# Window attention on one core: first batch in smaller pieces, the first strip's v masked by ScalarE, the projection turned later, and a wait moved from the pooled out to two other places

## The chip, the cores and the metric

The kernel runs on one core of a Trainium2 chip. The metric is the device time of one execution in microseconds (us). A core has five instruction queues: PE (TensorE), DVE (VectorE), ACT (ScalarE), POOL (GpSimd) and SP (SyncE, which here only issues DMAs). They run side by side and meet at semaphores.

## What is computed

The input x is (4, 128, 96, 96) float32. It goes through a group norm of 32 groups, then a linear attention over windows of 4x4 pixels, once on the windows and once on their 5x5 averages, and a projection with a batch norm; x is added at the end.

```python
qkv = jnp.einsum('nchw,oc->nohw', xw, qkv_w)            # xw: windows of 4x4 pixels
pooled = _avg_pool5(qkv)
msq = jnp.concatenate([qkv, pooled], axis=1)            # 32 heads of 3*8 channels
q, k, v = relu(msq[..., :8]), relu(msq[..., 8:16]), msq[..., 16:]
v = jnp.pad(v, ..., constant_values=1.0)                # the ones give the denominator
kv = jnp.einsum('ngld,nglm->ngdm', k, v)
out = jnp.einsum('ngld,ngdm->nglm', q, kv)
out = out[..., :-1] / (out[..., -1:] + 1e-15)
y = jnp.einsum('nchw,oc->nohw', out, proj_w)            # then the batch norm
x = x + y                                               # the attention gets _gn(x)
```

## The kernel before

Each of the 4 images of the batch is cut into 24 strips of four rows, so there are 96 strips (NS), each of 384 columns with the 128 channels on the partitions. All of x stays in x_all. SP loads batch 0 in six DMAs of four strips, then the constants and weights (all five on loaded_w), and the later batches two strips at a time.

**Head.** DVE takes the statistics of each strip as it lands (L453), and works out mean and reciprocal deviation in a chain of small operations (L461 to L488). It then normalises strip 0 (L517) and pools it (L509). POOL does both for strip 1 and every later strip (L286, L292, L264). ScalarE's two square roots (L407) serve this chain and the batch norm's scale (L629 to L637), by which DVE multiplies the projection's weights; PE turns these through PSUM (L811) and DVE copies them out to projT (L644). The columns of ones in vm_pool are written by DVE (L641), those of vm_full come with the DMA below.

**A strip's stages.** PE multiplies the normalised strip with the k and v weights (conv_kv, L659; for the pooled pixels conv_kv_pooled, L668) into PSUM banks 2, 3 and 6. ScalarE takes k out through a relu (relu_k L344, relu_k_pooled L349). v must stand in vm_full and vm_pool once per window of a quad, with zeros in the other windows' rows. For the full pixels ScalarE copies v once (copy_v, L355) and SP spreads it with four DMAs of every fourth row (spread_v, L234). For the pooled pixels ScalarE writes six masked copies, each with a column of constants as scale (masked_v_pooled, L366). PE then multiplies k with v (kv_products and kv_products_pooled, L687, in tiles of 64 rows and 32 columns), DVE copies the result out under a mask of own heads (own_heads, L561), PE multiplies with q (out_products and out_products_pooled, L703: 48 products of one strip each, that is 96 matmul records), DVE divides (L592 to L596), PE transposes (L778) and ScalarE copies out (L391, L398). In project PE multiplies with projT, first the full part (L787, bank 0) and then the pooled one (L789, bank 1). DVE adds the full part to x_all (residual, L567), ScalarE copies the pooled part to y_pool (copy_y_pooled, L403), between the second and third of the six masked copies, and POOL adds it (residual_pooled, L264). SP stores the strip.

**Order.** PE's step for strip s is written out by hand:

```python
conv_kv(s + 1, p); transposes(s - 1); conv_kv_pooled(s + 1, p)
project(s - 1, out_next=True)
out_products(s); out_products_pooled(s)
kv_products(s + 1); kv_products_pooled(s + 1)
conv_q(s + 1, p)
```

It stands in a hardware loop over strips 1 to 94, two to a turn, with strip 0 ahead of it and strip 95 behind. ScalarE's order in a step is relu_q, relu_q_pooled, copy_v, to_image, pooled_out, relu_k, relu_k_pooled, then the six masked copies. In the loop, out_products_pooled(s) begins with a wait for added_f (DVE has added the full part of strip s - 1) and y_copied (ScalarE has copied its pooled part) on an instruction that does nothing else. kv_products(s + 1), which writes banks 0 and 1, waits for vm_f alone. In twelve steps out of 96 DVE also has a part of the next batch's statistics between its own work (phases 0 to 3).

Of the kernel before, what the change touches and what calls it, by code (L numbers as in the profile page):

```python
# [11 lines left out]
P = 128  # L12
Q4 = 32
WS = 4
D = 8
# [21 lines left out]
C_TP = C_VP + EP  # L37
C_PACK = C_TP + EP
N_CONST = C_PACK + P


def constants():


    c = np.zeros((P, N_CONST), np.float32)
    p = np.arange(P)
    c[:, C_IDENT:C_IDENT + P] = np.eye(P)
    quad, head = p // Q4, p % Q4 // D
    for j in range(QG):
        at = C_OWN + j * KC  # L50
        c[:, at:at + KC] = (quad[:, None] % QG == j) & (head[:, None] == np.arange(KC)[None] // HC)
    win_p = p % Q4 // PXP
    side = np.array([1, 2, 1])
    times = (side[:, None] * side[None]).ravel()[p % Q4 % PXP][:, None]
    own_p = ((quad % QG * WP + win_p)[:, None] == np.arange(EP)[None]) & (win_p < WP)[:, None]
    c[:, C_VP:C_VP + EP] = own_p * times / 25.0
    c[:, C_TP:C_TP + EP] = own_p * times
    pads = p % Q4 >= WP * PXP
    c[np.concatenate([p[~pads], p[pads]]), C_PACK + p] = 1
    return c  # L60


def build(nc, x, wq, wkv, proj, bn, consts, out):
# [20 lines left out]
    with ExitStack() as ctx:  # L84
# [64 lines left out]
        loaded_w = sem("loaded_w")  # L149
        loaded_first = [sem(f"loaded_first{i}") for i in range(FOURS)]  # L150
        loaded_later = sem("loaded_later")
# [5 lines left out]
        pads_zero = sem("pads_zero")  # L157
        ones_set = sem("ones_set")
        mv_zero = sem("mv_zero")
        var_ready = sem("var_ready")  # L160
# [53 lines left out]
        def _(sp):  # L214
            for i in range(FOURS):
                sp.dma_start(x_all[:, 4 * i * SP:4 * (i + 1) * SP],
                             x_v[:, 0, 4 * i * SP:4 * (i + 1) * SP]).then_inc(loaded_first[i], 16)
            for dst, src in ((cst[:], consts), (wkv_sb[:], wkv), (wq_sb[:], wq), (bn_sb[:], bn), (proj_sb, proj)):
# [8 lines left out]
            def spread_v(s):  # L227


                sp.wait_ge(v_copied, s + 1)  # L230
                wait(sp, kv_f, s)
                for e in range(EF):
                    rows = slice(e, P, EF)
                    sp.dma_start(vm_full[rows, e], v_full[rows]).then_inc(vm_f, 16)  # L234
# [6 lines left out]

            spread_v(0)
            for s in range(NS):
# [11 lines left out]
        def _(pool):  # L255
# [72 lines left out]

            pool.wait_ge(pads_zero, 5)
            pool.wait_ge(dv_group, GS)  # L330
            normalise_and_pool(1, 1)
# [3 lines left out]
        def _(act):  # L335
# [16 lines left out]
            def copy_v(s):  # L352
                act.wait_ge(conv_f, s + 1)
                wait(act, vm_f, 16 * EF * s)
                act.activation(v_full[:].rearrange("p t (h c) -> p t h c", c=HC)[:, :, :, 0:D],  # L355
                               kv_tiles(KV_F, TF)[:, :, P:].rearrange("p t (h m) -> p t h m", m=D),
                               ACT.Copy).then_inc(v_copied, 1)

            def masked_v_pooled(s, between=None):

                act.wait_ge(conv_p, s + 1)
                wait(act, kv_p, s)
                heads = vm_pool[:].rearrange("p e t (h c) -> p e t h c", c=HC)
                src = kv_tiles(KV_P, TP)[:, :, P:].rearrange("p t (h m) -> p t h m", m=D)
                for e in range(EP):
                    last = act.activation(heads[:, e, :, :, 0:D], src, ACT.Copy, scale=col(C_VP + e))  # L366
                    if between is not None and e == 1:
                        copy_y_pooled(between)
                last.then_inc(vm_p, 1)
# [29 lines left out]

            def copy_y_pooled(s):  # L400
                act.wait_ge(y_p, s + 1)
                wait(act, y_done, s)
                act.activation(y_pool[:], ps[:, Y_P, 0:SPP], ACT.Copy).then_inc(y_copied, 1)  # L403
# [5 lines left out]
            square_root(0)  # L409
            square_root(1)  # L410
            act.wait_ge(loaded_w, 16 * 5)
# [19 lines left out]

            copy_v(0)
            relu_k(0)
            relu_k_pooled(0)
            masked_v_pooled(0)
# [7 lines left out]
        def _(dve):  # L443
# [88 lines left out]
            dve.wait_ge(mv_zero, 1)  # L532
            for i in range(FOURS):
                dve.wait_ge(loaded_first[i], 16)
                for at in range(4 * i, 4 * i + 4):
                    last = gather_strip(0, at)
                last.then_inc(gathered, 1)
            dve.wait_ge(gathered, FOURS)
# [99 lines left out]

            for e in range(EP):
                ones = vm_pool[:, e].rearrange("p t (h c) -> p t h c", c=HC)[:, :, :, D]  # L640
                last = dve.tensor_copy(ones, col(C_TP + e).unsqueeze(2).to_broadcast(list(ones.shape)))  # L641
            last.then_inc(ones_set, 1)
            dve.wait_ge(proj_turned, 1)
            dve.tensor_copy(projT[:], ps[:, TRF, 0:2 * P]).then_inc(projT_ready, 1)  # L644
            over_strips(step)
# [4 lines left out]
        def _(pe):  # L650
# [57 lines left out]
            def kv_products(s):  # L708

                if isinstance(s, int) and s < 2:  # L710
                    pe.wait_ge(km_f, s + 1)
                pe.wait_ge(vm_f, 16 * EF * (s + 1))
                pe.nop(nofuse=True)
# [32 lines left out]
            def out_products_pooled(s):  # L746
                if is_first(s):

                    pe.wait_ge(km_f, s + 2)
                    pe.nop(nofuse=True)  # L750
                elif is_last(s):
                    pe.wait_ge(kvc_p, s + 1)
                    pe.nop(nofuse=True)
                else:

                    pe.wait_ge(added_f, s)
                    pe.wait_ge(y_copied, s)
                    pe.nop(nofuse=True)
                for t in range(TP):
                    for e in range(WP):  # L760
                        last = out_tile(True, t, e)
                last.then_inc(out_p, 1)
# [19 lines left out]
            def project(s, out_next=False):  # L782
                pe.wait_ge(o_f, s + 1)
                if out_next:

                    out_wait(s + 1)
                pe.matmul(ps[:, Y_F, 0:SP], projT[:, 0:P], o_sb[:, 0:SP], start=True, stop=True).then_inc(y_f, 1)  # L787
                pe.wait_ge(o_p, s + 1)
                pe.matmul(ps[:, Y_P, 0:SPP], projT[:, P:2 * P], o_sb[:, SP:],  # L789
                          start=True, stop=True).then_inc(y_p, 1)  # L790
# [16 lines left out]
            conv_kv_pooled(0, 0)  # L807

            pe.wait_ge(proj_scaled, 1)
            for z in range(2):  # L810
                last = pe.transpose(ps[:, TRF, z * P:(z + 1) * P], proj_sb[:, z * P:(z + 1) * P], col(C_IDENT, P))  # L811
            last.then_inc(proj_turned, 1)

            pe.wait_ge(v_copied, 1)
            pe.wait_ge(km_f, 1)
            conv_kv(1, 1)
            pe.wait_ge(projT_ready, 1)
            pe.wait_ge(ones_set, 1)
            kv_products(0)
            kv_products_pooled(0)  # L820
            conv_q(0, 0)
# [39 lines left out]
```

## Time and profile before

| | |
|---|---|
| median of 3 runs | 886.83 us (884.42 to 887.57) |
| the profiled execution, its time | 886.18 us |
| its span, first to last instruction | 884.3 us |
| mean granted clock of TensorE | 0.998 |
| busy share PE, DVE, ACT, POOL | 96%, 79%, 54%, 75% |

The span is what the trace shows; 1.9 us of the execution's time lie around it. A row of a timeline begins with its start and its duration in us, and ends with the number of instructions that it merges and the idle time of its engine before them, where there was some. Matmul records overlap: each spans the way through the array, and the next begins long before it ends.

### The profile page before, as it was taken

The page shows a single profiled execution, that of the slowest core. Times are in us where ns is not written, and L with a number is a line of the kernel's source. Part 1 is how long each engine was busy: PE and PEld are TensorE (multiplying, and loading weights), DVE is VectorE, ACT ScalarE, POOL GpSimd, SP SyncE. Part 2 cuts the span into 40 slices and gives each one's busy share as a digit, 9 for nine tenths or more (in the row PEclk, how much of TensorE's full clock was granted, in tenths as well). Part 3 has the DMA queues.
Part 4 walks back from the last instruction along what each step waited for, and adds up shares of the span by engine and source line. Part 5 has one row for each costly group of instructions (what it writes and reads, how often), then busy time and mean ns, then how long its engine had stood idle before and what let it go on. Part 6 is the DMA issues. An engine that isn't in the chain of part 4 may idle for free.

```text
span 884.3 us, 63772 instructions
## 1 busy us (share of the span) xinstructions
PE 848.4 (96%) x28322; PEld 693.0 (78%) x28322; DVE 699.9 (79%) x1252; ACT 480.9 (54%) x1349; POOL 658.9 (75%) x1624
## 2 busy tenths in 40 slices
PE   0789999999999999999999999999999999999997
PEld 0568888888888888888888888888888888888885
DVE  7758888887778888888777888888777777777776
ACT  0346565646465655555555556565656564646563
POOL 2558787878787878777878777787878787878781
PEclk9999999999999999999999999999999999999999
DMA  6122322111123323111113232211111111111111
GB/s 236 40 77 81 103 84 82 49 47 48 47 69 97 91 94 98 51 48 47 49 50 99 86 98 88 82 51 48 48 50 46 49 48 47 48 47 48 47 49 47
DMA packets 39081, 60.06 MB, mean 68 GB/s; under 512 B 8560, under 2 KB 33648, under 8 KB 39024
## 3 DMA queue, kind: packets, MB, share of 16 engines
q1 hardware_dynamic: 39024, 59.52, 20.0%
q14 instruction: 48, 0.39, 0.1%
q8 instruction: 9, 0.15, 0.1%
HBM read 19.38 MB, written 18.87 MB: 43 GB/s over the span
## 4 chain that ended last, share of the span: by engine, by line
PE 94%; DVE 3%; issue 1%; DMA 1%; SPq 0%; ACT 0%; DVEq 0%
PE ps L703 24%; PE ps L687 17%; PE ps L659 14%; PE ps L668 9%; PE ps L675 9%; PE ps L787 7%; PE ps L778 6%; PE ps L789 4%; PE ps L676 4%; DVE stats L453 1%; DMA x_all<-x 0%; DVE kvc_full L561 0%; DVE kvc_pool L561 0%; DMA vm_full<-v_full 0%; DVE kvc_full L509 0%
## 5 line engine op out<-in xcount | busy, mean ns | idle before, releaser
L366 ACT ACTIVATE vm_pool<-ps,cst 128x256 f32<-128x256 f32 x576 | 230.1, 480 | 0.0
L376 ACT ACTIVATE q_full<-ps 128x384 f32<-128x384 f32 x96 | 47.2, 491 | 281.0 <-PE ps L675 281.0
L561 DVE TENSOR_TENSOR kvc_full<-ps,cst 128x864 f32<-128x864 f32 x192 | 193.2, 1048 | 4.7 <-PE ps L687 4.7
L561 DVE TENSOR_TENSOR kvc_pool<-ps,cst 128x864 f32<-128x864 f32 x192 | 193.2, 1048 | 0.5 <-PE ps L687 0.5
L286 POOL TENSOR_TENSOR xd<-x_all,mean_t 128x384 f32<-128x384 f32 x95 | 78.6, 827 | 154.3 <-PE ps L676 137.8
L659 PE MATMUL ps<-wkv_sb,xn 128*128 128x256 f32 x576 | 141.4, 382 | 23.1 <-DVE xn L517 23.1
L264 POOL TENSOR_TENSOR x_all<-y_pool,x_all 128x96 f32<-128x96 f32 x380 | 148.9, 424 | 12.7 <-DVE x_all L567 7.2
L659 PEld LDWEIGHTS ps<-wkv_sb,xn 128*128 128x128 f32 x576 | 109.4, 191 | 33.2 <-issue 23.0
L703 PEld LDWEIGHTS ps<-kvc_full,q_full 64*32 64x32 f32 x9216 | 108.3, 105 | 26.0 <-issue 26.0
L292 POOL TENSOR_TENSOR xn<-xd,rstd_t 128x96 f32<-128x96 f32 x380 | 121.8, 367 | 8.1 <-DVE xn L517 0.7
L703 PE MATMUL ps<-kvc_full,q_full 64*32 64x72 f32 x9216 | 125.0, 230 | 0.6 <-DVE kvc_pool L561 0.6
L703 PE MATMUL ps<-kvc_pool,q_pool 64*32 64x72 f32 x9216 | 116.1, 231 | 2.3 <-issue 2.2
L567 DVE SCALAR_TENSOR_TENSOR x_all<-ps,shift,x_all 128x384 f32<-128x384 f32 x96 | 59.3, 618 | 62.3 <-PE ps L787 57.7
L703 PEld LDWEIGHTS ps<-kvc_pool,q_pool 64*32 64x32 f32 x9216 | 101.8, 105 | 3.1 <-issue 3.0
L668 PE MATMUL ps<-wkv_sb,xp 128*128 128x256 f32 x384 | 99.7, 382 | 0.7 <-ACT q_pool L384 0.6
L687 PE MATMUL ps<-vm_full,k_full 64*32 64x144 f32 x4608 | 95.4, 288 | 2.3 <-issue 1.5
L687 PE MATMUL ps<-vm_pool,k_pool 64*32 64x216 f32 x3072 | 94.9, 345 | 1.9 <-issue 1.9
L264 POOL TENSOR_TENSOR hs<-ht,xn 128x96 f32<-128x96 f32 x190 | 84.0, 442 | 14.9
L355 ACT ACTIVATE v_full<-ps 128x384 f32<-128x384 f32 x96 | 47.3, 492 | 86.1 <-PE ps L659 86.0
L592 DVE TENSOR_SCALAR den_full<-ps 128x48 f32<-128x48 f32 x96 | 20.0, 208 | 90.1 <-PE ps L703 89.7
L675 PE MATMUL ps<-xn,wq_sb 128*128 128x384 f32 x192 | 87.6, 538 | 0.0
L787 PE MATMUL ps<-o_sb,projT 128*128 128x384 f32 x192 | 78.5, 491 | 0.0
(74 smaller groups left out, 1316.2 us busy)
## 6 DMA issues: line engine op xcount, KB each, us to landing
vm_full<-v_full SPq DMA_DIRECT2D x384, 54.0 KB, 1.9
out<-x_all SPq DMA_DIRECT2D x96, 192.0 KB, 1.9
x_all<-x SPq DMA_DIRECT2D x36, 384.0 KB, 3.4
x_all<-x SPq DMA_DIRECT2D x6, 768.0 KB, 7.9
cst<-consts SPq DMA_DIRECT2D x1, 170.0 KB, 11.0
wkv_sb<-wkv SPq DMA_DIRECT2D x1, 128.0 KB, 10.8
o_sb<-proj SPq DMA_DIRECT2D x1, 128.0 KB, 10.1
wq_sb<-wq SPq DMA_DIRECT2D x1, 64.0 KB, 10.6
```

The source lines that it names most:

```text
L264: return pool.tensor_tensor(o, a, b, ALU.add)
L286: link(pool.tensor_tensor(xd[:], x_all[:, s * SP:(s + 1) * SP], mean, ALU.subtract), 1)
L292: last = pool.tensor_tensor(xr[:, r], rows[:, r], rstd, ALU.mult)
L366: last = act.activation(heads[:, e, :, :, 0:D], src, ACT.Copy, scale=col(C_VP + e))
L561: last = dve.tensor_tensor(kvc[:, g], src.to_broadcast(shape), own, ALU.mult)
L567: dve.scalar_tensor_tensor(xs, ps[:, Y_F, 0:SP], shift[:], xs, ALU.add, ALU.add).then_inc(added_f, 1)
L659: last = pe.matmul(ps[:, bank, at:at + 2 * P], xn[:, p, t * P:(t + 1) * P], wkv_sb[:], start=True, stop=True)
L668: last = pe.matmul(ps[:, KV_P, t * 2 * P:(t + 1) * 2 * P], xp[:, p, t * P:(t + 1) * P], wkv_sb[:], start=True, stop=True)
L675: pe.matmul(ps[:, Q_F, 0:SP], wq_sb[:], xn[:, p], start=True, stop=True).then_inc(q_f, 1)
L687: last = pe.matmul(ps[Q4 * i:Q4 * (i + 1), bank + r, t * n:(t + 1) * n], k[rows, t, Q4 * i:Q4 * (i + 1)], vm[rows, :, t, i * KC:(i + 1) * KC],
L703: last = pe.matmul(ps[Q4 * c:Q4 * (c + 1), bank + g, t * n:(t + 1) * n], blocks[rows, 4 * t + c, Q4 * e:Q4 * (e + 1)], kvc[rows, r, w], st ...
L787: pe.matmul(ps[:, Y_F, 0:SP], projT[:, 0:P], o_sb[:, 0:SP], start=True, stop=True).then_inc(y_f, 1)
```

## The change

The first batch's six DMAs become nine: of 1, 1, 2, 4, 4, 4, 4, 2 and 2 strips. The ones of both vm_full and vm_pool are written by POOL, ten copies once the constants and weights have landed. For strip 0 ScalarE writes v masked into vm_full, four times with a column of new constants (C_VF) as scale; the copy and the four DMAs fall away for this strip, and the second square root moves behind strip 0's relu of k. PE multiplies strip 1 with the k and v weights, then k with v of strip 0, and only then turns the projection, into bank 7. In the loop, the wait for added_f and y_copied in front of the pooled out goes: y_copied is waited for in front of kv_products instead, added_f by ScalarE ahead of its copy of the pooled part, which moves behind the third masked copy, and km_f (k of strip s + 1 is taken out) by PE between the two matmuls of project.

```diff
+        pieces = [1, 1, 2] + [4] * (FOURS - 2) + [2, 2]
-            for i in range(FOURS):
-                sp.dma_start(x_all[:, 4 * i * SP:4 * (i + 1) * SP],
-                             x_v[:, 0, 4 * i * SP:4 * (i + 1) * SP]).then_inc(loaded_first[i], 16)
+            at = 0
+            for i, n in enumerate(pieces):
+                sp.dma_start(x_all[:, at:at + n * SP], x_v[:, 0, at:at + n * SP]).then_inc(loaded_first[i], 16)
+                at += n * SP
@@ spread_v(s), SP
-                sp.wait_ge(v_copied, s + 1)
+                sp.wait_ge(v_copied, s)
-            spread_v(0)
@@ POOL
+            pool.wait_ge(loaded_w, 16 * 5)
+            for vm, n, first_col in ((vm_full, EF, C_VF), (vm_pool, EP, C_TP)):
+                for e in range(n):
+                    ones = vm[:, e].rearrange("p t (h c) -> p t h c", c=HC)[:, :, :, D]
+                    last = pool.tensor_copy(ones, col(first_col + e).unsqueeze(2).to_broadcast(list(ones.shape)))
+            last.then_inc(ones_set, 1)
@@ ACT
+            def masked_v_first():
+                act.wait_ge(conv_f, 1)
+                act.wait_ge(ones_set, 1)
+                ...
+                for e in range(EF):
+                    last = act.activation(heads[:, e, :, :, 0:D], src, ACT.Copy, scale=col(C_VF + e))
+                last.then_inc(vm_first, 1)
-                    if between is not None and e == 1:
+                    if between is not None and e == 2:
                         copy_y_pooled(between)
             def copy_y_pooled(s):
                 act.wait_ge(y_p, s + 1)
+                act.wait_ge(added_f, s + 1)
-            square_root(1)
-            copy_v(0)
+            masked_v_first()
             relu_k(0)
+            square_root(1)
@@ DVE
-            for e in range(EP):
-                ones = vm_pool[:, e].rearrange("p t (h c) -> p t h c", c=HC)[:, :, :, D]
-                last = dve.tensor_copy(ones, col(C_TP + e).unsqueeze(2).to_broadcast(list(ones.shape)))
-            last.then_inc(ones_set, 1)
             dve.wait_ge(proj_turned, 1)
-            dve.tensor_copy(projT[:], ps[:, TRF, 0:2 * P]).then_inc(projT_ready, 1)
+            dve.tensor_copy(projT[:], ps[:, Q_F, 0:2 * P]).then_inc(projT_ready, 1)
@@ kv_products(s), PE
-                pe.wait_ge(vm_f, 16 * EF * (s + 1))
+                if is_first(s):
+                    pe.wait_ge(vm_first, 1)
+                else:
+                    pe.wait_ge(vm_f, 16 * EF * s)
+                wait(pe, y_copied, s - 1)
@@ out_products_pooled(s), PE, where s is neither the first nor the last
-                    pe.wait_ge(added_f, s)
-                    pe.wait_ge(y_copied, s)
-                    pe.nop(nofuse=True)
@@ project(s, out_next), PE
                 pe.wait_ge(o_p, s + 1)
+                if out_next:
+                    pe.wait_ge(km_f, s + 3)
                 pe.matmul(ps[:, Y_P, 0:SPP], projT[:, P:2 * P], o_sb[:, SP:],
@@ PE, head
-            pe.wait_ge(proj_scaled, 1)
-            ... the two transposes into bank TRF ...
-            pe.wait_ge(v_copied, 1)
+            pe.wait_ge(vm_first, 1)
             pe.wait_ge(km_f, 1)
             conv_kv(1, 1)
-            pe.wait_ge(projT_ready, 1)
-            pe.wait_ge(ones_set, 1)
             kv_products(0)
+            pe.wait_ge(proj_scaled, 1)
+            ... the two transposes into bank Q_F ...
             kv_products_pooled(0)
+            pe.wait_ge(projT_ready, 1)
             conv_q(0, 0)
```

## Rows read from the trace of the kernel before

**Rows 1.** PE's waits: us in total, times, longest

```profile
PE ps L659 <- DVE xn L517: 23.1, 1, 23.1
PE ps L687 <- issue: 3.4, 2, 1.9
PE ps L703 <- issue: 2.2, 1, 2.2
```

**Rows 2.** The tile x_all, first 30 us: issues, then time to landing

```profile
L216 SPq DMA_DIRECT2D x_all<-x x6: 386/438/715, 0.7 to 3.4; - x6
L517 DVE TENSOR_SCALAR xn<-x_all,mean_t,rstd_t x4: 359/373/882, 21.3 to 22.6; 128x96 f32<-128x96 f32 x4
DMA to landing us min/median/max: 4.4/7.9/11.2
```

**Rows 3.** Timeline of the head

```profile
5.20 11.29 DVE L453 BATCH_NORM_STATS2 stats<-x_all 128x6 f32<-128x384 f32 x24 [4.31 <-DMA x_all<-x]
...
21.45 0.90 POOL L286 TENSOR_TENSOR xd<-x_all,mean_t 128x384 f32<-128x384 f32 x1 [16.46 <-DVE rstd_t L488]
...
23.08 2.90 PE L659 MATMUL ps<-wkv_sb,xn 128*128 128x256 f32 x6 [23.08 <-DVE xn L517]
...
26.40 0.48 ACT L355 ACTIVATE v_full<-ps 128x384 f32<-128x384 f32 x1
...
26.78 0.48 ACT L344 ACTIVATE k_full<-ps 128x384 f32<-128x384 f32 x1
...
26.91 0.35 POOL L264 TENSOR_TENSOR vt<-hs 128x72 f32<-128x72 f32 x1
...
28.33 0.20 PEld L811 LDWEIGHTS ps<-cst,o_sb 128*128 128x128 f32 x2 [0.84 <-DVE o_sb L637]
...
28.61 1.46 PE L659 MATMUL ps<-wkv_sb,xn 128*128 128x256 f32 x6
28.88 0.41 DVE L644 COPY projT<-ps 128x256 f32<-128x256 f32 x1
...
30.85 0.98 PE L687 MATMUL ps<-vm_full,k_full 64*32 64x144 f32 x48 [0.78 <-DMA vm_full<-v_full]
...
31.91 2.02 DVE L561 TENSOR_TENSOR kvc_full<-ps,cst 128x864 f32<-128x864 f32 x2 [2.63 <-PE ps L687]
```

**Rows 4.** Timeline of one step of the loop

```profile
305.42 0.51 ACT L344 ACTIVATE k_full<-ps 128x384 f32<-128x384 f32 x1
...
305.98 0.51 PEld L789 LDWEIGHTS ps<-o_sb,projT 128*128 128x128 f32 x2
...
306.30 0.53 PE L789 MATMUL ps<-o_sb,projT 128*128 128x216 f32 x2
306.50 0.62 DVE L567 SCALAR_TENSOR_TENSOR x_all<-ps,shift,x_all 128x384 f32<-128x384 f32 x1
...
306.76 1.32 PE L703 MATMUL ps<-kvc_full,q_full 64*32 64x72 f32 x96
306.86 0.35 ACT L403 ACTIVATE y_pool<-ps 128x216 f32<-128x216 f32 x1
...
307.86 1.20 PE L703 MATMUL ps<-kvc_pool,q_pool 64*32 64x72 f32 x96
```

**Rows 5.** Timeline of strip 0's step, then of one with statistics (from 385 us)

```profile
36.01 1.20 PE L703 MATMUL ps<-kvc_full,q_full 64*32 64x72 f32 x96 [0.58 <-DVE kvc_pool L561]
...
37.00 1.20 PE L703 MATMUL ps<-kvc_pool,q_pool 64*32 64x72 f32 x96
...
385.54 1.31 PE L703 MATMUL ps<-kvc_full,q_full 64*32 64x72 f32 x96
...
386.14 0.62 DVE L567 SCALAR_TENSOR_TENSOR x_all<-ps,shift,x_all 128x384 f32<-128x384 f32 x1
...
386.90 1.20 PE L703 MATMUL ps<-kvc_pool,q_pool 64*32 64x72 f32 x96
```

**Rows 6.** Windows 60 to 65 us: PE, PEld, DVE, ACT, POOL busy, granted clock

```profile
60.00:65.00 5.00, 3.56 (x117) 2.72 (x117) 2.19 (x5) 0.00 (x0) 1.19 (x4) 0.67 0.29 106
```

More of the change, by code:

```diff
@@ L37 @@
 C_TP = C_VP + EP
-C_PACK = C_TP + EP
+C_VF = C_TP + EP
+C_PACK = C_VF + EF
 N_CONST = C_PACK + P
@@ L57, in constants @@
     c[:, C_TP:C_TP + EP] = own_p * times
+    c[:, C_VF:C_VF + EF] = p[:, None] % EF == np.arange(EF)[None]
     pads = p % Q4 >= WP * PXP
@@ L149, in build @@
         loaded_w = sem("loaded_w")
-        loaded_first = [sem(f"loaded_first{i}") for i in range(FOURS)]
+        pieces = [1, 1, 2] + [4] * (FOURS - 2) + [2, 2]
+        assert sum(pieces) == SPB
+        loaded_first = [sem(f"loaded_first{i}") for i in range(len(pieces))]
         loaded_later = sem("loaded_later")
@@ L158, in build @@
         ones_set = sem("ones_set")
+        vm_first = sem("vm_first")
         mv_zero = sem("mv_zero")
@@ L353, in copy_v @@
                 act.wait_ge(conv_f, s + 1)
-                wait(act, vm_f, 16 * EF * s)
+                wait(act, vm_f, 16 * EF * (s - 1))
                 act.activation(v_full[:].rearrange("p t (h c) -> p t h c", c=HC)[:, :, :, 0:D],
@@ L357, in copy_v @@
                                ACT.Copy).then_inc(v_copied, 1)
+            def masked_v_first():
+                act.wait_ge(conv_f, 1)
+                act.wait_ge(ones_set, 1)
+                heads = vm_full[:].rearrange("p e t (h c) -> p e t h c", c=HC)
+                src = kv_tiles(KV_F, TF)[:, :, P:].rearrange("p t (h m) -> p t h m", m=D)
+                for e in range(EF):
+                    last = act.activation(heads[:, e, :, :, 0:D], src, ACT.Copy, scale=col(C_VF + e))
+                last.then_inc(vm_first, 1)
             def masked_v_pooled(s, between=None):
@@ L532, in _ @@
             dve.wait_ge(mv_zero, 1)
-            for i in range(FOURS):
+            at = 0
+            for i, n in enumerate(pieces):
                 dve.wait_ge(loaded_first[i], 16)
-                for at in range(4 * i, 4 * i + 4):
+                for at in range(at, at + n):
                     last = gather_strip(0, at)
-                last.then_inc(gathered, 1)
+                    if at % 4 == 3:
+                        last.then_inc(gathered, 1)
+                at += 1
             dve.wait_ge(gathered, FOURS)
@@ L746, in out_products_pooled @@
             def out_products_pooled(s):
-                if is_first(s):
-                    pe.wait_ge(km_f, s + 2)
-                    pe.nop(nofuse=True)
[L751 to L754, printed above, removed]
-                    pe.wait_ge(added_f, s)
-                    pe.wait_ge(y_copied, s)
+                if is_first(s) or is_last(s):
+                    if is_first(s):
+                        pe.wait_ge(km_f, s + 2)
+                    else:
+                        pe.wait_ge(kvc_p, s + 1)
                     pe.nop(nofuse=True)
@@ L807, in _ @@
             conv_kv_pooled(0, 0)
+            pe.wait_ge(vm_first, 1)
+            pe.wait_ge(km_f, 1)
+            conv_kv(1, 1)
+            kv_products(0)
             pe.wait_ge(proj_scaled, 1)
             for z in range(2):
-                last = pe.transpose(ps[:, TRF, z * P:(z + 1) * P], proj_sb[:, z * P:(z + 1) * P], col(C_IDENT, P))
+                last = pe.transpose(ps[:, Q_F, z * P:(z + 1) * P], proj_sb[:, z * P:(z + 1) * P], col(C_IDENT, P))
             last.then_inc(proj_turned, 1)
-            pe.wait_ge(v_copied, 1)
-            pe.wait_ge(km_f, 1)
-            conv_kv(1, 1)
+            kv_products_pooled(0)
             pe.wait_ge(projT_ready, 1)
-            pe.wait_ge(ones_set, 1)
-            kv_products(0)
-            kv_products_pooled(0)
             conv_q(0, 0)
```

## The prediction

> **What bounds the kernel.** PE is busy for 96% of the span, so the first question is what its 4% of idle time is. I read PE's waits first [rows 1]: 23.1 us are the head, before its first product, and 3.4 + 2.2 us are three pauses that the trace puts down to issue, with no semaphore behind them; a further 0.78 us before the first kv product is a wait for the DMA that spreads v [rows 3]. In the loop PE waits for nobody for long. So there are two places where this change can act: the head, where a chain of DVE work sets when PE starts, and PE's own row in the loop, where a saving has to come from the handing over between two groups of matmuls. A hundredth of a microsecond per strip makes 0.9 us.
>
> Then the head by its tile view and timeline [rows 2, 3]. The reader is to see what each step of the chain ends on: DMAs, then 24 statistics, then small DVE operations, then PE and ScalarE in turn. Last a step of the loop by its timeline [rows 4], to see which of the waits that move has slack.
>
> **Smaller loads.** The first piece of four strips lands at 0.73 + 4.4 = 5.1 us, the last at 3.4 + 11.2 = 14.6 [rows 2]; that is 1.9 us per piece. DVE takes 11.29 / 24 = 0.470 us per strip, 1.88 for four [rows 3]. The two run at one pace, so DVE stands at the last landing with four strips left and ends at 14.6 + 1.88 = 16.5, as the row says. With the new pieces DVE starts up to 1.5 us earlier, but then waits for the pieces of four in the middle. The one that ends with strip 20 lands at 5.1 + 4 x 1.9 = 12.7, and eight strips follow: 12.7 + 8 x 0.47 = 16.46. The early start is thus lost in the middle, and the two last pieces of two save nothing, since DVE has work left when they land. Gain 0.03 us. Three more issues at 0.44 us each lie on SP, which is ahead of the data. Bounds: -0.1, and +0.3 if the first small pieces use the DMA engines less well; the weights, behind them, are needed only at 23 us.
>
> **Ones by POOL.** POOL is idle for 16.46 us up to 21.45 [rows 3]. The constants and weights, 492 KB, follow x at its pace (768 KB in 1.9 us), 14.6 + 1.2 = 15.8. Ten copies of 48 or 32 elements per partition end well ahead: POOL's addition of 72 took 0.35 us, its subtraction of 384 took 0.90 [rows 3]. What they can cost is DVE's time: they run just beside the chain of small operations that sets the head. When POOL ran its 0.90 us subtraction, one DVE operation on data in SBUF took 882 ns where its neighbours took 359 to 379 [rows 2, 3], so 0.5 us were lost on 0.9 us of POOL work. Ten copies of between 0.1 us (as many elements as the subtraction in all) and 0.25 us (two thirds of the addition) are 1 to 2.5 us of such work; the loss lies between 0 and 1.4 us. I take 0.2, because most of these copies end before DVE has left its long last step of the statistics, and the operations behind it are small. The six copies that DVE sheds lay behind the chain and pay nothing.
>
> [...]
>
> **First strip's v, and the projection.** Before, ScalarE's copy (26.40), the relu of k (26.78, done 27.26) and four DMAs led to the kv product at 30.85, of which 0.78 us were waited for the DMA behind strip 1's conv product [rows 3]. After, the four masked copies start when PE's first product ends (23.08 + 2.90 = 25.98) at 26.03. A copy of 384 columns is followed by the next after 0.38 us and lasts 0.48 [rows 3], so four take 1.5 to 1.9 us; I take 1.84, since the scale is now a column. k is out at 26.03 + 1.84 + 0.48 = 28.35, and strip 1's conv product, which writes over both, starts at 28.5 + 0.1 with its wait: 28.6 instead of 28.61. It lasts 1.46 us, so kv starts at 30.0 or 30.1, some 0.8 us earlier. Then the gain is lost: DVE reaches own_heads only after projT, which now is turned behind the kv product. DVE's own_heads began 31.91 - 30.85 = 1.06 us after kv's start, which gives 31.1; from the weight load of the transposes to the copy it was 28.88 - 28.33 = 0.55, the copy takes 0.41 + 0.03. So 31.1 + 0.55 + 0.44 = 32.1 instead of 31.9. PE's product with q waits for both halves of own_heads. Cost 0.15 us, bounds -0.25 (ScalarE's copies at 0.38) to +0.5 (ScalarE later still, with the square root and the scale of the projection behind it). Without the DMA nothing else in the head becomes late: the spread of strip 1 waits for the kv product, as before.
>
> **The wait in front of the pooled out.** In the loop's step the pooled out's first matmul starts 307.86 - 306.76 = 1.10 us after the full out's [rows 4]. The full out's records, 1.32 us merged, run on 0.22 us past the pooled out's first matmul: no idle time can be read at the place of this wait. ScalarE had its copy out at 307.21 and DVE its addition at 307.12, 0.65 us before. The wait is met; what can be saved is the handling of one instruction. Bounds: nothing; and 0.10 us per step, which is how much longer the full out takes here than in strip 0's step, 37.00 - 36.01 = 0.99 [rows 5], where the wait has fixed numbers. That step does have a wait at this place too, so most of the 0.10 must be something else. I take 0.015 us, 94 times: -1.4 us (0 to -9.4).
>
> In the steps with statistics the wait does bind: from the full out to the pooled one it is 386.90 - 385.54 = 1.36 us, and DVE's addition ends only at 386.76 [rows 5]. Removing it is worth up to 0.26 us in each of three batches; I count 0.6, since the wait need not be as long in all of them. ScalarE now takes this wait, half a microsecond ahead of its last three masked copies; the pooled kv product that needs them comes behind the pooled out and the full kv product, some 2 us later. So -0.6 us (0 to -0.8).
>
> **What is added in the loop.** ScalarE's wait for the addition: the copy's new place is one masked copy later, 306.86 + some 0.38 = 307.24, and the addition ends at 307.12, so it is met. y_pool is ready at 307.6 instead of 307.2; POOL's queue has strip s + 2's pooling ahead of it, and the wait for y_copied in front of kv_products comes behind the pooled out, at 307.86 + 1.1 = 309.0. The wait for k between project's two matmuls is tighter: k is out at 305.42 + 0.51 = 305.93, and the weight load behind the wait starts at 305.98. But the matmul starts only at 306.30 and one of the two loads in 0.51 us takes 0.19, so the load may start as late as 306.1. Cost 0. If this cover were gone each 0.1 us would be 9 us in all.
>
> **Sum.** -0.03 + 0.2 + 0.15 - 1.4 - 0.6 = -1.7 us, on the profiled execution's 886.18: 884.5. The median shown is 0.65 higher, 886.83, from which it is 885.1. I predict 885.0.
>
> **Rivals.**
> A: the removed instruction costs PE its full handling. For it: the full out is 0.10 us longer in the loop than at strip 0. Against it: no gap at its place. 94 x 0.10 = 9.4 instead of 1.4: 877.
> B, the other side: the wait for k binds. It decides as soon as the load starts over 0.18 us after the relu's end (306.1 against 305.93). For it: only 0.05 us between that end and the load today. Against it: the matmul ahead covers the rest. At 0.1 us a step +9.4: 894.
> C: POOL's copies and ScalarE's later hand-over take more of the head, +1.4 and +0.5 at their bounds: 887, no change.
> D: the three issue pauses and the clock. [...] One pause with its clock is worth 2.2 + 1.6 = 3.8 us. A shifted head may remove or add one: 881.2 or 888.8.
>
> [...]
>
> **Chances.** The forecast (883 to 887) 0.50, A 0.14, B 0.08, C 0.13, D 0.15, half to each side. A measurement of this kernel tells about 0.5%, 4.4 us, from no change. Faster by more: A, half of D and a tail of the forecast, 0.26; slower by more: B, 0.08; within: 0.66. The range leaves out most of A and all of B: 880.0 to 888.8.
>
> **What would show it.** Statistics end at 16.4 to 16.8 and the first xn operation starts at 21.3 to 21.6; the DVE operations from 16.5 to 20 us are longer only where POOL copies run. The kv product of strip 0 starts at 30.0 and own_heads at 32.1. In the loop, from full out to pooled out is 1.08 to 1.10 us: 1.00 would be A. Project's second matmul starts 0.65 us after its first, or later for B. The step at 385 us has lost its 0.26. I am wrong if the period of a step moves by more than 0.03 us, or if the pauses of the first 65 us change.

## The result

| | before | after |
|---|---|---|
| median of 11 runs | 886.26 us (884.42 to 887.62) | 890.54 us (887.69 to 892.50) |
| profiled: its time, span | 886.18, 884.3 | 891.37, 889.6 |
| granted clock | 0.998 | 0.994 |

The ratio is 1.0045, 95% interval 1.0032 to 1.0058: 4 us slower, where I predicted 885.0 and a range up to 888.8. Three places of the profile after show the loss.

**The loads.** The tile x_all, first 30 us, answers to [rows 2]:

```profile
L477 DVE BATCH_NORM_STATS2 stats<-x_all x24: 541/543/561, 3.4 to 18.0; 128x6 f32<-128x384 f32 x24
L223 SPq DMA_DIRECT2D x_all<-x x9: 386/432/1332, 0.7 to 5.5; - x9
L541 DVE TENSOR_SCALAR xn<-x_all,mean_t,rstd_t x4: 354/364/976, 23.4 to 24.7; 128x96 f32<-128x96 f32 x4
...
DMA to landing us min/median/max: 2.5/8.4/11.6
```

The head's timeline, answering to [rows 3]:

```profile
3.36 1.02 DVE L477 BATCH_NORM_STATS2 stats<-x_all 128x6 f32<-128x384 f32 x2 [2.46 <-DMA x_all<-x]
...
6.80 1.02 DVE L477 BATCH_NORM_STATS2 stats<-x_all 128x6 f32<-128x384 f32 x2 [2.42 <-DMA x_all<-x]
...
9.18 9.39 DVE L477 BATCH_NORM_STATS2 stats<-x_all 128x6 f32<-128x384 f32 x20 [1.37 <-DMA x_all<-x]
18.25 0.75 POOL L340 COPY vm_full<-cst 128x48 f32<-128x48 f32 x4 [13.26 <-DMA o_sb<-proj]
...
18.89 0.99 POOL L340 COPY vm_pool<-cst 128x32 f32<-128x32 f32 x6
...
25.26 2.90 PE L682 MATMUL ps<-wkv_sb,xn 128*128 128x256 f32 x6 [25.26 <-DVE xn L541]
...
28.33 1.99 ACT L378 ACTIVATE vm_full<-ps,cst 128x384 f32<-128x384 f32 x4 [5.92 <-PE ps L682]
...
30.20 0.51 ACT L356 ACTIVATE k_full<-ps 128x384 f32<-128x384 f32 x1
...
32.27 0.99 PE L710 MATMUL ps<-vm_full,k_full 64*32 64x144 f32 x48
33.19 0.20 PEld L841 LDWEIGHTS ps<-cst,o_sb 128*128 128x128 f32 x2 [0.23 <-issue]
...
34.01 2.01 DVE L588 TENSOR_TENSOR kvc_full<-ps,cst 128x864 f32<-128x864 f32 x2
```

DVE starts 1.84 us earlier than before, but then waits twice more for data, 2.42 + 1.37 = 3.79 us, and its statistics end at 9.18 + 9.39 = 18.57 instead of 16.49. From there to PE's first product both kernels take nearly the same (6.69 and 6.59 us). The strips that DVE waits for come late; the windows of 3 to 4 and 4 to 5 us say how (busy time of PE, PEld, DVE, ACT and POOL, then PE's clock, the DMA engines' busy share, GB/s), before:

```profile
3.00:4.00 1.00, 0.00 (x0) 0.00 (x0) 0.00 (x0) 0.00 (x0) 1.00 (x2) 1.00 1.02 412
4.00:5.00 1.00, 0.00 (x0) 0.00 (x0) 0.00 (x0) 0.00 (x0) 0.99 (x2) 1.00 1.00 418
```

and after:

```profile
3.00:4.00 1.00, 0.00 (x0) 0.00 (x0) 0.64 (x2) 0.00 (x0) 1.00 (x2) 1.00 0.86 169
4.00:5.00 1.00, 0.00 (x0) 0.00 (x0) 0.38 (x1) 0.00 (x0) 0.99 (x2) 1.00 0.85 277
```

The engines are less busy by a seventh only (0.86 and 0.85), and move 169 and 277 GB/s instead of 412 and 418. From 2 to 3 us it was the other way round, 303 against 172. The last piece lands at 16.73 us instead of 14.53.

**The pauses of PE.** Its waits, answering to [rows 1]:

```profile
PE ps L682 <- DVE xn L541: 25.3, 1, 25.3
PE ps L726 <- issue: 4.9, 2, 2.6
PE ps L710 <- issue: 2.3, 2, 2.0
```

The head takes 2.2 us more, the pauses put down to issue are 7.2 us instead of 5.6, and there is one more of them. The chain of waits shows where it is, in strip 0's pooled out (start, duration, what):

```profile
38.10 1.41 PE ps L726 x82
39.51 2.64 issue
42.15 1.45 PE ps L726 x76
```

The kernel before had 2.19 us of products in one row there, and its first pause behind them:

```profile
36.01 2.19 PE ps L703 x128
38.21 0.80 PE ps L687 x48
39.01 1.87 issue
```

**The clock.** Windows 40 to 45 and 45 to 50 us after, which answer to [rows 6]:

```profile
40.00:45.00 5.00, 2.85 (x127) 2.48 (x127) 1.56 (x5) 0.00 (x1) 1.48 (x5) 0.56 0.01 3
45.00:50.00 5.00, 4.70 (x43) 2.74 (x38) 4.04 (x4) 0.85 (x2) 0.37 (x1) 0.50 0.01 3
```

The clock falls inside the new pause, and from 40.7 to 50.9 us, 10.2 us long, PE is granted half of it (0.50); before, the one such stretch was 3.4 us (61.7 to 65.1). So the profiled 5.3 us are 2.1 of head, 1.6 of pauses and up to 6.8 / 2 = 3.4 of clock, less 1.1 that the loop gives back. With 3.4 these make 6.0, so the clock's part is nearer 2.7.

One profile is one draw of this. Half-clock stretches come and go between executions of one kernel, and each execution's mean granted clock is on record. Of the 35 executions of the kernel before that stand beside e5, ten had 1.000 and took 885.45 us in the median, and 18 had 0.998 and took 887.12: 0.002 of mean clock go with 1.7 us. The mean over executions was 0.9984 before (the 31 beside e1) and 0.9956 after. At that rate, which makes it an estimate, 2.4 of the 4 us are clock.

**The loop.** A common step, answering to [rows 4], and the step with statistics of [rows 5]:

```profile
312.68 1.24 PE L726 MATMUL ps<-kvc_full,q_full 64*32 64x72 f32 x91
313.69 0.24 PE L726 MATMUL ps<-kvc_pool,q_pool 64*32 64x72 f32 x1
...
314.85 0.98 PE L710 MATMUL ps<-vm_full,k_full 64*32 64x144 f32 x48
...
391.50 1.23 PE L726 MATMUL ps<-kvc_full,q_full 64*32 64x72 f32 x93
...
393.63 0.98 PE L710 MATMUL ps<-vm_full,k_full 64*32 64x144 f32 x48
```

From full to pooled out is now 1.01 us instead of 1.10, which I had named as the sign of rival A. It isn't: up to the next kv product it is 314.85 - 312.68 = 2.17 us, and before it was 2.19:

```profile
308.95 0.98 PE L687 MATMUL ps<-vm_full,k_full 64*32 64x144 f32 x48
...
388.00 0.98 PE L687 MATMUL ps<-vm_full,k_full 64*32 64x144 f32 x48
```

The pooled out starts among the full out's last products, and PE hardly does more work per time. In the step with statistics the same stretch fell from 388.00 - 385.54 = 2.46 to 2.13 us. Over 88 steps the mean period went from 8.772 to 8.760 us, worked out from the records of the pooled convolution. With the loop's waits alone (e3 below) it is 8.764.

### The profile page after: what moved, and what is told of

Read it like the earlier page. It is cut to its first block, busy times and chain, and to the rows that moved or that the text cites. A ratio compares the mean times of both kernels' runs of the same rounds, so it can differ in the third digit from the quotient of the medians.

```text
span 889.6 us, 63778 instructions
## 1 busy us (share of the span) xinstructions
PE 850.7 (96%) x28322; PEld 691.0 (78%) x28322; DVE 700.7 (79%) x1246; ACT 482.6 (54%) x1352; POOL 659.9 (74%) x1634
## 4 chain that ended last, share of the span: by engine, by line
PE 94%; DVE 3%; issue 1%; DMA 1%; SPq 0%; DVEq 0%; ACT 0%
PE ps L726 24%; PE ps L710 17%; PE ps L682 14%; PE ps L691 9%; PE ps L698 9%; PE ps L810 7%; PE ps L801 6%; PE ps L814 4%; PE ps L699 4%; DVE stats L477 1%; DMA x_all<-x 1%; DVE kvc_full L588 0%; DVE kvc_pool L588 0%; DVE kvc_full L533 0%; DVE xn L541 0%
## 5 line engine op out<-in xcount | busy, mean ns | idle before, releaser
L726 PE MATMUL ps<-kvc_pool,q_pool 64*32 64x72 f32 x9216 | 121.8, 232 | 4.9 <-issue 4.9
L726 PEld LDWEIGHTS ps<-kvc_pool,q_pool 64*32 64x32 f32 x9216 | 104.7, 105 | 5.7 <-issue 5.7
```

The costliest lines, as they stand in the source:

```text
L726: last = pe.matmul(ps[Q4 * c:Q4 * (c + 1), bank + g, t * n:(t + 1) * n], blocks[rows, 4 * t + c, Q4 * e:Q4 * (e + 1)], kvc[rows, r, w], st ...
```

## The experiments

e4 has 8 executions and each other experiment 12, set against the 29 to 35 of the kernel before that were taken with it. All records of PE counted (weight loads, matmuls, semaphore and the few control instructions), it has one long pause behind record 705 of its trace and one behind record 1217 in all twenty kernels (0.86 to 2.9 us from start to start), and the additional one is behind record 449: they are 256 and 512 records apart. In each of these pauses the last packet of kind "instruction" on DMA queue 8, of 16384 bytes, had ended 1.1 to 1.7 us before PE went on. From this I take it that PE gets its program in blocks of 256 such records, one packet each. Below, a border is the edge of such a block and a fetch its packet. "Late" is the time to the next packet from the start of PE's 194th record, the first of the block that ends with record 449; the pause is that in strip 0's pooled out, from the chain of waits. The length of PE's program is counted in the compiled kernel, where an f32 product counts once (in the trace it is two weight loads and two matmuls: the 48 products of an out have 96 matmul records). The trace has the difference of one: up to record 449 it shows eight semaphore instructions of PE in each kernel with 643 and nine in each with 644.

| run | PE's program | late, us | pause, us | median, us | ratio (95%) |
|---|---|---|---|---|---|
| before | 644 | 0.55 | none | | |
| after | 643 | 5.5 | 2.64 | 890.54 | 1.0045 (1.0032, 1.0058) |
| e1 | 643 | 6.0 | 2.91 | 888.01 | 1.0023 (1.0006, 1.0040) |
| e2 | 644 | 0.71 | none | 888.02 | 1.0018 (1.0002, 1.0033) |
| e3 | 644 | 0.56 | none | 885.95 | 0.9994 (0.9982, 1.0005) |
| e4 | 643 | 5.2 | 2.02 | 890.07 | 1.0042 (1.0029, 1.0055) |
| e5 | 643 | 5.1 | 2.36 | 886.00 | 0.9998 (0.9986, 1.0009) |
| e6 | 643 | 4.5 | 2.10 | 887.08 | 1.0008 (0.9995, 1.0022) |
| e7 | 643 | 6.0 | 2.91 | 889.18 | 1.0024 (1.0010, 1.0038) |
| e8 | 644 | 1.3 | none | 886.63 | 1.0000 (0.9985, 1.0015) |
| e9 | 643 | 5.5 | 2.36 | 888.12 | 1.0015 (0.9997, 1.0032) |
| e10 | 644 | 0.55 | none | 886.05 | 0.9995 (0.9980, 1.0010) |
| e11 | 644 | 0.55 | none | 885.72 | 0.9991 (0.9976, 1.0005) |
| e12 | 644 | 0.70 | none | 888.24 | 1.0017 (0.9999, 1.0035) |
| e13 | 644 | 0.64 | none | 888.59 | 1.0026 (1.0013, 1.0038) |
| e14 | 644 | 0.56 | none | 886.36 | 1.0001 (0.9988, 1.0014) |
| e15 | 643 | 5.5 | 2.55 | 889.16 | 1.0028 (1.0014, 1.0041) |
| e16 | 644 | 3.2 | 0.44 | 885.79 | 0.9993 (0.9975, 1.0011) |
| e17 | 643 | 5.7 | 2.81 | 888.88 | 1.0028 (1.0014, 1.0043) |
| e18 | 644 | 3.2 | 0.44 | 884.92 | 0.9979 (0.9963, 0.9994) |

### The parts apart: e1 to e4

e1: the changed kernel with the old loads.

```diff
-        pieces = [1, 1, 2] + [4] * (FOURS - 2) + [2, 2]
+        pieces = [4] * FOURS
```

> The changed kernel with the first batch loaded again in six pieces of four strips. Theory L (the small pieces are what costs: in the changed kernel the statistics end at 18.57 us instead of 16.5): they end at 16.5 again, q's first product for strip 0 starts at 36.0 to 36.2 instead of 38.1, and the time falls by at least 2.1 us, to below 888.5. Theory H (the new order of the head moves the program so that PE's issue pauses come at worse places, 4 us): the head falls by 2.1 us, but the long pause in strip 0's pooled out with its half clock stays, and the time is some 888.4, still slower than before. Theory L with pauses that follow the late head: 884 to 885.5, no slower than before.

e2: the kernel before with the nine pieces.

> The kernel before with the nine pieces alone. Theory L: statistics end 2 us later, time +2.1 us (888.4), or +4 and more (890 to 891) if PE's pauses grow with it. Theory H: +2.1 us and PE's pauses as in the kernel before, 1.9, 1.5 and 2.2 us long.

e3: the kernel before with the loop's waits of the change (copy_y_pooled, kv_products, out_products_pooled, project). e4: e1 with the loop's waits as before.

> The kernel before with the loop's waits moved and nothing else. By the periods of the two traces (8.772 us before, 8.760 after) it is 1.1 us faster: 885.2. Rival (the wait for k costs what the other saves): 886.3. The pauses in the first 65 us as before.

> The changed kernel with six pieces of four strips and with the loop's waits as before: the first strip's masked v, POOL's ones and the later projection alone. Theory L: 886.0 to 886.8, own_heads of strip 0 at 31.9 to 32.1 us, so nothing gained and nothing lost. Theory H: 888 to 891, with the first pause in strip 0's pooled out.

The loads cost 0.22% on the changed kernel (1.0045 to 1.0023, 1.9 us, though the two intervals overlap) and 0.18% on the one before (1.6 us, interval just clear of 1). The loop's waits give 0.06% of before (the interval holds 1) and 0.19% of e4, whose interval overlaps that of e1. So their gain is small at most. The new head costs 0.42%, and in e1 and e4, as in the changed kernel, PE has the additional pause.

### Loads by size: e8 and e12

```diff
+        pieces = [2] * 12                      # e8
+        pieces = [1, 1, 2] + [4] * (FOURS - 1) # e12
```

> The kernel before with the first batch in twelve pieces of two strips. If any piece under four strips slows the landings (in e2_loads_only they came 0.6 to 2 us late from the third on, which was of two strips): statistics end 1.5 to 3 us later than 16.5, time 888 to 889.5. If only the two pieces of one strip do it: the pace of 1.9 us per four strips holds, DVE ends one strip's time behind the last landing, at 15.6 to 16.0 us, and the time is 885.4 to 885.8.

> The kernel before with the first four strips in pieces of one, one and two, and the last four in one piece as before (seven pieces). Theory (the small pieces at the front start the transfers at a worse pace, and the two at the end merely shift along): the last piece lands 1.2 to 1.6 us later than before (15.7 to 16.1 instead of 14.53), the statistics end 1.3 to 1.7 us later, ratio 1.0015. Rival (the loss comes with the number of pieces, nine against six, each costing about 0.5 us): last landing 15.1, ratio 1.0005.

e8's last piece lands at 15.5 us, 1.0 later than before's 14.5, but only two strips follow it instead of four, and its statistics end at 16.58, as before's 16.49. So twelve DMAs cost the landings 1 us and the kernel nothing, and e8 lies between its two forecasts. e12 (eight pieces, not the seven of its expectation) has its last landing at 15.9, and PE's wait for its first product is 24.5 instead of 23.1 us. What e12 has and e8 has not is the two pieces of one strip at the front. The window of 3 to 4 us of e12:

```profile
3.00:4.00 1.00, 0.00 (x0) 0.00 (x0) 0.66 (x2) 0.00 (x0) 1.00 (x2) 1.00 0.98 172
```

It isn't the short lines that are slow. From 2 to 4 us e12's packets of 1536 bytes (a strip's line per partition) took 65 to 71 ns each, some 22 bytes a ns, where before's packets of 6144 bytes took 244 ns from 3 to 4 us, 25 bytes a ns. But the packets of 3072 bytes that begin beside them took 372 ns each in this window, and 123 ns in e8. Why they do is open.

### What delays the program block: e5, e6, e7, e9, e10

The chain of waits calls the pause "issue". The DMA view shows the packets of kind "instruction". In before the first one behind record 194 lies between 32.3 and 34.0 us:

```profile
q8 instruction: 1, 0.02, 4.7%
```

After, there is none from 32.0 to 39.4 us; the window of 39.4 to 41.0 us has it:

```profile
q8 instruction: 1, 0.02, 5.5%
```

It starts at 39.52, takes 1.4 us, and PE goes on at 42.15, 1.2 us behind its end; in the eight other kernels with this pause it is 1.3 to 1.4 us. In all nine kernels with the additional pause the packet starts from 0.1 us before to 0.8 us after the last weight load ahead of the pause, that is, when PE has come to the end of its block; in the eleven others it starts 2.0 to 4.7 us ahead of that record. Three guesses at its delay first, all on e1: the next batch's loads a strip later (e5), the wait for projT ahead of the pooled kv product (e6), strip 1's spread behind the kv products (e7).

```diff
-                if b + 1 < B and 2 * t < SPB:              # e5, SP
-                    load_two(b + 1, 2 * t)
+                if b + 1 < B and 0 <= t - 1 and 2 * (t - 1) < SPB:
+                    load_two(b + 1, 2 * (t - 1))
+            pe.wait_ge(projT_ready, 1)                     # e6, PE
             kv_products_pooled(0)
-            pe.wait_ge(projT_ready, 1)
+                if s == 1:                                 # e7, SP, spread_v
+                    sp.wait_ge(kv_p, 1)
```

> As e1_after_old_loads (the changed kernel with six pieces of four), and each of the later batches' loads of two strips is issued one step later, so that none is under way in strip 0's step. There PE paused 2.9 us in the pooled out of strip 0, for a block of its program whose fetch began only at 38.0 us, 6.0 us after PE had entered the block before it; in the kernels with the old head that fetch begins 0.6 us after. Theory Q (the fetch stands behind the data DMAs: the spread of v and the load of 384 KB issued at 34.1): without the load the fetch begins at some 35.5 us, ahead of need, the pause in the pooled out is 0 to 0.5 us and the time 885.5 to 886.5. Theory W (PE's wait for projT_ready just behind the block's boundary keeps the fetch back): the pause stays, 2 to 3 us, and the time is 888.

> As e1_after_old_loads, but PE waits for projT_ready ahead of the pooled kv product of strip 0 instead of behind it, so no semaphore wait stands at the block's boundary. Theory W: the fetch begins within 1 us of the boundary, as with the old head, no pause in strip 0's pooled out, 885.5 to 886. Theory Q: the spread is then even further ahead of the boundary, the fetch begins at 37.5 to 38.5 us again, the pause stays at 2 to 3 us, 888.3.

> As e1_after_old_loads, but SP issues the spread of strip 1's v only when the pooled kv product of strip 0 is done (some 32.4 us instead of 31.65), that is behind the moment in which PE enters the block (32.0). Theory Q in its form as a race (a fetch asked for ahead of the spread's data goes at once, one asked for behind them waits until they have drained): the fetch begins at 32.5 to 33, no pause in the pooled out, 885.5 to 886. If the order of the two doesn't matter: the fetch at 38 to 39 us, pause of 2 to 3 us, 888.

All three keep the pause, so neither these loads nor that wait nor a spread ahead of the border delays the packet. e5 was 2 us faster than e1 all the same (its interval and that of e1 overlap a little). e11 asks whether that gain stands by itself: it is e3, the kernel before with the loop's waits moved, with the loads of e5. The forecast was 884.0 if the small gains add up, and 885.5 to 886.5 if not. It took 885.72, and its interval holds 1, so the later loads gave nothing clear there. Then the position in the program:

```diff
             conv_kv(1, 1)
+            pe.nop(nofuse=True)                            # e9, on e1
             kv_products(0)
-            pe.wait_ge(ones_set, 1)                        # e10, on before
```

> The changed kernel with six pieces of four strips and one empty instruction more on TensorE, ahead of the first strip's full kv products, so that every later product stands where it stood in the program of the kernel before, against the borders at which TensorE's issue pauses. Theory of position (the additional pause in strip 0's pooled out comes with the shift of the program by one instruction): no pause of 2 us or more in strip 0's pooled out, the other pauses of 1 to 2.5 us stay, and the time is 885.2 to 886.5 us, ratio 0.999 to 1.000. Rival, order of work (it is the new order of the head that delays that fetch, wherever it stands): the pause stays at 2.0 to 2.9 us and the time is 887.5 to 888.5, ratio 1.002.

> The kernel before with one instruction fewer on TensorE: its wait for the ones ahead of the first full kv products is left out (the wait for the turned projection, which VectorE writes after the ones, covers it). Everything behind then stands one place earlier in TensorE's program, as in the changed kernel, and the order of the head is the old one. Theory of position: the pause of 2.0 to 2.9 us appears in strip 0's pooled out, and the time is 888 to 889, ratio 1.002. Rival, order of work: no such pause, 885.8 to 886.8, ratio 1.000.

Both showed what the theory of position did not expect, and I took it to be refuted. But neither edit had moved anything: the program of e9 has 643 instructions like e1's (the lone empty instruction isn't in it), that of e10 644. PE's semaphore instructions have one or two waits each in the traces: before has 384 with one and 195 with two, e10 385 and 194, so e10 only left one wait alone in its pair.

### The head's parts: e13, e14, e15

e13: e1 with the projection turned at its old place. e14: before with it turned late. e15: e1 with the second root early.

> The changed kernel with six pieces of four strips and the projection turned at its old place (ahead of strip 1's kv convolution, into the old bank); the first strip's v still masked by ScalarE, ones by GpSimd, second square root later. Theory T (turning the projection behind the full kv products is what makes TensorE's next program block come 4 to 6 us late): that block is fetched 0.5 to 1.3 us after its predecessor is entered, no pause in strip 0's pooled out, time 885.2 to 886.6, ratio 0.999 to 1.000. Theory V (the masking by ScalarE, with no spread by DMA ahead of the first kv products, is what does it): fetch 4.5 to 6 us after, pause of 2.0 to 2.9 us there, 887.5 to 888.5, ratio 1.002.

> The kernel before with one part of the change alone: the projection turned behind the first strip's full kv products, through the other bank. Theory T: the fetch comes 4.5 to 6 us late, the pause of 2.0 to 2.9 us appears in strip 0's pooled out, time 887.8 to 888.8, ratio 1.002. Theory V: no such pause, 885.8 to 886.8, ratio 1.000.

> The changed kernel with six pieces of four strips and the second batch's square root back at its place ahead of the first strip's copies. Theories T and V both: the pause stays, 887.5 to 888.5, ratio 1.002. Rival S (the root between the first strip's copies moves ScalarE's later work and with it the fetch): no pause in strip 0's pooled out, 885.2 to 886.6, ratio 0.999 to 1.000. The root takes 0.2 us on ScalarE and is off the path either way.

Neither T nor V by itself: e13 and e14 are both free of the pause, and e15 has it. e13 is slow for another reason. Its transposes wait for the scale behind the later square root, and the clock is at its half from 31.0 to 34.4 us behind that wait (its 12 executions had a mean granted clock of 0.9958):

```profile
30.48 0.44 PE L837 MATMUL ps<-cst,o_sb 128*128 128x128 f32 x2 [2.53 <-DVE o_sb L664]
```

So in the changed kernel the root can only be late because the transposes are. What all kernels with the pause had in common was the count, 643.

### One instruction: e16, e17, e18

```diff
             conv_kv(1, 1)
+            pe.wait_ge(pads_zero, 5)                       # e16, on e1: a third wait
             kv_products(0)
-                if isinstance(s, int) and s < 2:           # e17, on before, kv_products
+                if isinstance(s, int) and s == 1:
-            pe.wait_ge(ones_set, 1)
```

e18 is e16 with the loads of e5. By then it was eight kernels with 643 and nine with 644.

> The changed kernel with six pieces of four strips and one more wait of TensorE, on zeroed pads (long since set), ahead of the first strip's full kv products. It makes three waits there out of two, and the compiled program holds one semaphore instruction more in front of them; TensorE's program then has 644 instructions, as the kernel before and all kernels without the additional pause have, and not 643, as all with it have (the empty instruction of an earlier run was dropped in compiling, and the wait taken out in another was one of a pair, so that neither of them moved anything). Theory of position: the next block is fetched within 1.3 us of its predecessor's entry, no pause in strip 0's pooled out, time 885.0 to 886.4, ratio 0.998 to 1.000. Rival, order of work: fetch 4.5 to 6 us after, pause 2.0 to 2.9 us, 887.5 to 889, ratio 1.002.

> The kernel before with two waits fewer in front of the first strip's full kv products (the one for the ones, and a second one for k, both covered by waits that stay), so that its semaphore instructions there are one instead of two and TensorE's program has 643 instructions; nothing else differs. Theory of position: the next block is fetched 4.5 to 6 us after its predecessor's entry, a pause of 2.0 to 2.9 us appears in strip 0's pooled out, time 888 to 889, ratio 1.0015 to 1.003. Rival, order of work: no such pause, 885.8 to 886.8, ratio 1.000.

> The kernel of the first of these three runs, and the loads of later batches issued one strip later: six pieces, the new head with one semaphore instruction more, the loop's waits moved. Theory: without the pause and with the loop's -0.9 us it takes 884.0 to 885.5, ratio 0.997 to 0.999, the lowest of all. Rival: the head and the place of the half-clock stretches give the gain back, 886 to 887, ratio 1.000.

The chain of waits of e17, which is the kernel before but for two satisfied waits:

```profile
35.65 1.41 PE ps L703 x81
37.06 2.81 issue
39.88 1.06 PE ps L703 x63
```

and of e16:

```profile
35.90 1.40 PE ps L726 x79
37.30 0.44 issue
37.74 1.06 PE ps L726 x64
```

One instruction fewer made the kernel before slower by 0.28% (2.5 us), clear of 1; one more took 1.0023 to 0.9993 (2.7 us), where the two intervals overlap a little. For the pause itself position is shown from both sides. The trace shows the shift: with 643 the border falls ahead of a weight load, which in the changed kernel starts only at 42.15; with 644 it falls between a weight load and its matmul (in e16 the load starts at 37.03, its matmul at 37.74). The order of work has a part: in e16 and e18 the packet still starts 3.2 us late, where the old head has 0.5 to 1.3, against the forecast of 1.3 at most and no pause; 0.44 us of pause are left. What starts a fetch in time was not found. e18 is the fastest of all, 0.21% under before.

What the pause costs in time varies. e5, e6 and e9 have it and their intervals hold 1, and e13 is 0.26% slower without it. Part of the price is the clock: the mean granted clock over the executions was 0.9967 in e17 against 0.9982 of before beside it, and 0.9967 in e1 against 0.9984 in e16. At the rate above, an estimate, 1.3 and 1.4 us of the 2.5 and 2.7 are clock. But half-clock stretches also come without this pause: the profiled executions of e3, e10, e12 and e13 have two of 3.4 us each.

## Why the prediction was wrong

- **Smaller loads, -0.03: failed.** The step "the one that ends with strip 20 lands at 5.1 + 4 x 1.9" took the first four strips to land at 5.1 in any cut. In three pieces they landed at 6.77, and the whole row was late with them: the piece that ends with strip 20 landed at 14.77 instead of 12.7, and 14.77 + 8 x 0.47 = 18.53 is where the statistics ended (18.57). That is +2.1 us in the profile, 1.6 to 1.9 by the runs. The pace of the later pieces (1.9 us each from 9.16 us on) and the eight strips that follow were right. My bound for pieces that use the engines less well, +0.3, had no row behind it.
- **Ones by POOL, +0.2:** it was 0, and for another reason than mine. I had most copies end before the statistics do, since the weights would land at 15.8. They landed at 18.1, behind the late pieces, and the copies ran at 18.25 to 19.88, nearly all beside DVE's small operations. From the end of the statistics to the first xn operation it is 4.84 us, before 4.85. My 0.2 did not come.
- **First strip, +0.15:** against PE's first product kv starts 7.01 us later instead of 7.77 (0.76 gained, 0.8 said), and own_heads 8.75 instead of 8.83. The gain of the kv product was nearly lost again at own_heads, as I had it. What is left is -0.1 where I had +0.15: the other sign, inside the bounds.
- **Wait of the pooled out, -1.4, and the phase steps, -0.6:** the period's 0.012 us make -1.1 in all. The three longest steps give 0.14 each of it (9.04 to 8.90), 0.4; 0.7 is left for the others, 0.007 a step and not 0.015. A is refuted: its 0.10 us a step are not there. So is B: with the wait for k the second matmul of project starts 0.67 us after the first in the mean over all steps, before 0.65, and the period fell all the same.
- **Rival D was the other half of the loss,** in kind and roughly in size: 2.5 to 2.7 us by e17 and e16, where I had 3.8 for one pause with its clock. The 1.6 of clock in it was an estimate from the 0.67 of [rows 6] (3.3 of 5 us at half the clock, half of that lost), and no run shows it by itself; by the rate above, also an estimate, the clock was 1.3 and 1.4 us of the 2.5 and 2.7. The forecast itself put this at nothing, and my own sign of being wrong, that the pauses of the first 65 us change, came. I gave its slower half 7 in 100, since I held that a shift of PE's program by one instruction or so would leave the pauses as they are, for which no row stood. That took a border's place for the whole matter. Whether the block is there in time is another question than where it begins, and one instruction decided it. The border at record 449 cost no pause before and 2.81 us in e17, and up to 2.91 (e1).

The terms by the runs: loads +1.9 (after less e1), pause with its clock +2.7 (e1 less e16), what is left of head and loop -0.6 (e16 less before), sum +4.0. The sum is the measured one by the way it is made, and proves nothing by itself; the check from the other side is e2 with 1.6 and e17 with 2.5.

## What to carry to other kernels

Count the instructions of an engine's program in both kernels before reading anything into an order of work: here one semaphore instruction more (e16) or fewer (e17) moved all that follows against a fetch border, and the time by 2.7 and 2.5 us. It showed in the straight code ahead of the loop, 37 to 39 us into the span; between 71 and 873 us no run has a packet of kind "instruction" on queue 8. Check in the compiled program that an experiment on position has moved something. Cutting a first transfer small can bring its first piece earlier and all behind it later: here pieces of one strip brought the first by 1.84 us, and the statistics ended 2.1 us later. Read the moved GB/s beside the engines' busy share.

## What the runs showed of the hardware

- One border of PE's program cost between 0 and 2.9 us, by a shift of one instruction (0 before, 2.81 in e17; 2.91 in e1, 0.44 in e16). In the first 75 us of the profiled executions with this pause the clock was at its half for 6.8 to 10.2 us, in those without it for 0 to 6.8 us.
- From 3 to 4 us the DMA engines at a busy share of 0.98 to 1.02 moved 172 GB/s with packets of 1536 and 3072 bytes (e12), 390 with packets of 3072 bytes alone (e8) and 412 with packets of 6144 (before).
- POOL's small copies (0.75 us for four, 0.99 for six) slowed no DVE operation on small data beside them (0.80, 0.21 and 0.19 us as before). Beside its subtraction of 384 columns one of DVE's four xn operations again took long (976 ns, the others from 354).
